# Decay exponents of a chunked scan: from TensorE matmuls to sums broadcast by DMA and clamped on GpSimd, with weight casts on ScalarE

## The reference

```python
proj = hidden_states @ in_proj_w.T
gate, xBC, dt = jnp.split(proj, [INTER, INTER + CONV_DIM], axis=-1)
xBC = silu(causal_conv_4_taps(xBC) + conv_b)
x, Bm, Cm = jnp.split(xBC, ...)
dt = jnp.clip(softplus(dt + dt_bias), DT_MIN, DT_MAX)
A = -jnp.arange(1, H + 1)
cs = jnp.cumsum(dt * A, axis=-1)              # within a chunk
Lmat = jnp.where(tri, jnp.exp(cs[l] - cs[s]), 0.0)
scores = (C[l] . B[s]) * Lmat
Ydiag = scores @ (x * dt)
# the second chunk also gets the first chunk's part, decayed by
# exp(cs_first[end] - cs_first[s]) * exp(cs_second[l])
Y = Ydiag + Yoff + x * D
yg = Y * silu(gate)
out = (yg / rms_per_group(yg)) * norm_w
return out @ out_proj_w.T
```

## Time and profile before

| What | Value |
| --- | --- |
| median of 3 runs | 2436.57 us (2436.28 to 2437.01) |
| time of the profiled execution | 2438.06 us |
| span of the profiled execution | 2436.3 us |
| TensorE busy | 2246.3 us, 92% |
| VectorE busy | 1789.6 us, 73% |
| ScalarE busy | 983.2 us, 40% |
| GpSimd busy | 842.5 us, 35% |
| the 64 units of stage C | about 695 to 2173 us of the span |

### The profile page before, as it was taken

How to read it: one execution, slowest core, us unless ns; L and a number is a source line. 1 busy time by engine, 2 the same in 40 slices (tenths; PEclk the granted TensorE clock), 3 DMA queues, 4 the chain that set the end, 5 groups by cost and what they waited for, 6 DMA issues and landing times. The chain is left out here.

```text
span 2436.3 us, 35643 instructions
## 1 busy us (share of the span) xinstructions
PE 2246.3 (92%) x11269; PEld 1731.1 (71%) x11333; DVE 1789.6 (73%) x2628; ACT 983.2 (40%) x1535; POOL 842.5 (35%) x481
## 2 busy tenths in 40 slices
PE   7888689979999999999999999999999999985987
PEld 5776568767867777776777777777777777764865
DVE  5433354448878887888888888888888888877887
ACT  2322111114344454554554455454455555431222
POOL 5424034321133443444335335334434435330000
PEclk9999889989999999999999999999999999996999
DMA  5413230012221111010111111111010110102433
GB/s 191 169 47 134 62 117 0 0 40 83 100 76 41 43 38 41 27 53 27 41 49 31 41 40 41 39 41 41 27 53 28 39 53 27 41 5 91 142 112 108
DMA packets 61935, 145.13 MB, mean 60 GB/s; under 512 B 15726, under 2 KB 18944, under 8 KB 61312
## 3 DMA queue, kind: packets, MB, share of 16 engines
q1 hardware_dynamic: 61888, 144.53, 18.0%
HBM read 133.74 MB, written 10.75 MB: 59 GB/s over the span
## 5 line engine op out<-in xcount | busy, mean ns | idle before, releaser
L70 PE MATMUL bank<-xT_hi,C_w_hi 128*128 128x512 f32 x1160 | 480.0, 414 | 13.4 <-POOL C_w_lo L1390 6.7
L71 PE MATMUL bank<-xT_lo,C_w_hi 128*128 128x512 f32 x1160 | 460.5, 397 | 0.0
L72 PE MATMUL bank<-xT_hi,C_w_lo 128*128 128x512 f32 x1160 | 459.9, 396 | 0.0
L1355 POOL TENSOR_TENSOR C_w_lo<-C_raw,C_w_hi 128x512 fp32r<-128x512 f32 x130 | 172.2, 1325 | 580.5 <-DVE C_w_hi L1182 530.1
L1109 DVE SCALAR_TENSOR_TENSOR C_acc<-bank,C_par,C_acc 128x510 f32<-128x510 f32 (+2 forms) x384 | 285.6, 747 | 68.9 <-ACT C_acc L1423 43.5
L1509 ACT ACTIVATE C_decay<-bank 128x512 f32<-128x512 f32 x384 | 215.8, 597 | 262.8 <-PE bank L1656 132.1
L1222 DVE TENSOR_TENSOR C_group_out<-bank,C_group_out 128x512 f32<-128x512 f32 x256 | 175.0, 684 | 176.6 <-PE bank L72 176.0
L1231 DVE TENSOR_TENSOR C_decay<-C_decay,C_cb 128x512 f32<-128x512 f32 x384 | 291.9, 789 | 4.2 <-DMA C_cb<-cb_rows 2.5
L70 PEld LDWEIGHTS bank<-xT_hi,C_w_hi 128*128 128x128 f32 x1160 | 219.3, 189 | 79.2 <-issue 10.8
L72 PEld LDWEIGHTS bank<-xT_hi,C_w_lo 128*128 128x128 f32 x1160 | 219.2, 189 | 53.2
L71 PEld LDWEIGHTS bank<-xT_lo,C_w_hi 128*128 128x128 f32 x1160 | 219.5, 189 | 48.1
(11 more groups left out here) (236 smaller groups left out, 4437.5 us busy)
## 6 DMA issues: line engine op xcount, KB each, us to landing
C_raw<-in_Cxg SPq DMA_DIRECT2D x65, 512.0 KB, 3.5
C_raw_out<-in_Cout SPq DMA_DIRECT2D x64, 256.0 KB, 3.4
D_raw<-in_D SPq DMA_DIRECT2D x32, 512.0 KB, 3.8
A_raw<-in_A SPq DMA_DIRECT2D x20, 512.0 KB, 5.9
A_stat_raw<-in_D SPq DMA_DIRECT2D x16, 512.0 KB, 3.5
D_raw<-in_D SPq DMA_DIRECT2D x32, 256.0 KB, 2.6
cb_rows<-C_decay SPq DMA_DIRECT2D x8, 768.0 KB, 3.3
C_cb<-cb_rows SPq DMA_DIRECT2D x8, 768.0 KB, 4.4
```

What stands on the lines that cost most here:

```text
L70: pe.matmul(out, lh, rh, start=start, stop=False)
L71: pe.matmul(out, lh, rl, start=False, stop=False)
L72: return pe.matmul(out, ll, rh, start=False, stop=stop)
L1355: e.tensor_tensor(w_lo[:, slot, :], raw_at, f32(w_hi[:, slot, :]), ALU.subtract).then_inc(lo_done, 1)
```

## The change

- The running sums cs (float32, 128 heads by 1024 tokens) are stored once in DRAM. For each unit one DMA (`load_cs`) reads the two heads' rows and writes them to all 128 partitions, 1 MB, into one of two buffers `cs_all`. The three small loads are gone.
- TensorE's exponent rounds, the mask matmuls and the bf16 parts are gone. GpSimd computes min(cs[l] - cs[s], 0) in 16 pieces of 128x128 per unit (`clamp`), straight into `decay`. For the first chunk against the second, ScalarE takes the broadcast sums with a bias per partition (8 Exp of 128x128); of the clamped pieces it makes 4 Exp of 128x512, in place. The mask is multiplied into the C.B blocks when they are made, once per group.
- GpSimd's low part of the x weights now stands inside `clamp`, after the wait for `inside` of the same unit.
- The three weight casts go from VectorE to ScalarE. ScalarE's exponentials stand ahead of the gate's Silu, and it copies the unit's own sums (`sums`).
- `turn` writes banks 6 and 7 and stands after the first output tile; `x_steps` stands after the first `out_add`. `in_g` waits for the gate's Silu of the unit before in place of `x_steps`.
- Before the units, three more transposes (of cs and of the sums to a chunk's end) and their copies, and five pieces in place of three in `move_cb`; the making of the bf16 parts is gone.

```diff
-        cs_rows = nc.dram_tensor("cs_rows", (P, 3, N), BF16, kind="Internal").ap()
-        cs_cols = nc.dram_tensor("cs_cols", (P, BATCH, 3, SEQ), BF16, kind="Internal").ap()
-        end_rows = nc.dram_tensor("end_rows", (P, 3, N), BF16, kind="Internal").ap()
+        cs_rows = nc.dram_tensor("cs_rows", (HEADS, N), F32, kind="Internal").ap()
...
-        left = sb("left", [P, 2, SEQ], BF16)
-        right = sb("right", [P, N], BF16)
-        fill = sb("fill", [P, 2 * SEQ], BF16)
+        cs_t = sb("cs_t", [P, CHUNKS, HEADS + 2])
+        cs_two = sb("cs_two", [P, 2, CHUNKS, 2])
+        end_t = sb("end_t", [P, BATCH, HEADS])
+        cs_all = sb("cs_all", [P, 2, 2 * N])
...
-            def load_rows(u):
-                heads = bass.ds(u.U * 2, 2)
-                wait(sp, S.seg_mm, u.U * ROUNDS)
+            def load_cs(u):
+
                 if u.first:
-                    sp.wait_ge(S.parts_out, 80)
-                    sp.wait_ge(S.fills_in, 128)
-                sp.dma_start(right[18:24, :], cs_rows[heads, :, :].rearrange("h a t -> (h a) t")).then_inc(S.rows_in, 16)
-                sp.dma_start(right[0:6, :], end_rows[heads, :, :].rearrange("h a t -> (h a) t")).then_inc(S.rows_in, 16)
-                sp.dma_start(left[6:18, :, :], cs_cols[heads, :, :, :].rearrange("h b a t -> (b a) h t"))\
-                  .then_inc(S.rows_in, 16)
+                    sp.wait_ge(S.cs_out, 16)
+                if not u.first_pair:
+                    sp.wait_ge(S.decays, (u.U - 1) * EXPS)
+                sp.dma_start(cs_all[:, u.j, :].rearrange("p (h t) -> p h t", h=2),
+                             cs_rows[bass.ds(u.U * 2, 2), :].unsqueeze(0).broadcast_to([P, 2, N])).then_inc(cs_in[u.j], 16)
...
-                for r in range(3):
-                    if r == 2:
-                        v.wait_ge(S.cb_mm, 2 * g + 2)
-                    v.tensor_copy(e[:, r, :], bank[4 + r][:, :]).then_inc(S.cb_moved, 1)
+                for bp in range(2):
+                    own = lambda t, c: t.rearrange("p (b c l) -> p b c l", b=2, c=2)[:, :, c, :]
+                    v.scalar_tensor_tensor(out=own(e[:, bp, :], 0), in0=mask[:, 0:2 * P].rearrange("p (b l) -> p b l", b=2),
+                                           scalar=0.0, in1=own(bank[4 + bp][:, :], 0), op0=ALU.is_ge, op1=ALU.mult)\
+                     .then_inc(S.cb_moved, 1)
+                    v.tensor_copy(own(e[:, bp, :], 1), own(bank[4 + bp][:, :], 1)).then_inc(S.cb_moved, 1)
+                v.wait_ge(S.cb_mm, 2 * g + 2)
+                v.scalar_tensor_tensor(out=e[:, 2, :], in0=mask[:, :], scalar=0.0, in1=bank[6][:, :],
+                                       op0=ALU.is_ge, op1=ALU.mult).then_inc(S.cb_moved, 1)
...
-                                bank[2 + h][:, :].rearrange("p (c h q) -> p c h q", c=4, h=2),
+                                bank[6 + h][:, :].rearrange("p (c h q) -> p c h q", c=4, h=2),
...
-                x_weights(U + 1, 1 - s)
-                if u.j == 0 and not u.first:
-                    out_weights(u)
...
-                gate_weights(U + 1, 1 - s)
+                x_steps(u, 0)
+                x_steps(u, 1)
                 if out:
                     out_add(u, 1)
                 decay_round(u, 0)
                 if out:
                     out_add(u, 2)
                 decay_round(u, 1)
+                decay_round(u, 4)
                 if out:
                     out_add(u, 3)
                 decay_round(u, 2)
-                x_steps(u, 0)
-                x_steps(u, 1)
                 decay_round(u, 3)
-                decay_round(u, 4)
                 decay_round(u, 5)
                 if u.group_ends:
                     mean_square(u, g)
-                if u.j == 1:
-                    out_weights(u)
             for_units(v, body)
-            out_weights(last)
             y_low(last.V - 1, 0, 1)
             for h in range(2):
...
+            def clamp(u):
+                wait(e, S.y_mm, u.U * 2)
+                if u.first:
+                    e.wait_ge(S.cb_stored0, 8 * GROUPS)
+                    e.wait_ge(S.cb_stored1, 8 * GROUPS)
+                e.wait_ge(S.sums_copied, u.U + 1)
+                e.wait_ge(cs_in[u.j], (u.U - u.j) * 8 + 16)
+                low(S.x_w_hi, 0, raw[:, 1 - u.j, 0:D], S.x_w_lo, u.U + 2)
+                for h in range(2):
+                    for c in range(2):
+                        for b in range(BATCH):
+                            at = N * h + SEQ * b + CHUNK * c
+                            to = decay[:, 4 + h, P * b:P * (b + 1)] if c else \
+                                decay[:, 2 * h + b // 2, SEQ * (b % 2):SEQ * (b % 2) + CHUNK]
+                            e.tensor_scalar(to, cs_all[:, u.j, at:at + CHUNK], cs_two[:, u.j, 2 * b + c, h:h + 1],
+                                            0.0, ALU.subtract, ALU.min).then_inc(S.clamped, 1)
             def body(u):
                 U, s = u.U, u.j
-                low(S.x_w_hi, 0, raw[:, 1 - s, 0:D], S.x_w_lo, U + 2)
                 if u.j == 0 and not u.first:
                     out_low(u)
+                clamp(u)
...
+            def chunk_ends():
+                a.wait_ge(S.dt_chain_v, DT_V)
+                for b in range(BATCH):
+                    t = SEQ * b
+                    a.activation(ends[:, CHUNK * b:CHUNK * (b + 1)], cs[:, t:t + CHUNK], ACT.Identity, scale=-1.0,
+                                 bias=cs[:, t + CHUNK - 1:t + CHUNK]).then_inc(S.dt_chain_a, 1)
+            def x_weights(U, slot):
+                a.wait_ge(raw_in[slot], (U - slot) * 8 + 16)
+                wait(a, S.in_x, U * 2)
+                a.activation(w_hi[:, 0, :], raw[:, slot, 0:D], ACT.Copy).then_inc(S.x_w_hi, 1)
+            def gate_weights(U, slot):
+                wait(a, S.in_g, U * 2)
+                a.activation(w_hi[:, 1, :], raw[:, slot, D:2 * D], ACT.Copy).then_inc(S.g_w_hi, 1)
+            def out_weights(u):
+                a.wait_ge(raw_out_in[1 - u.j], (u.V - (1 - u.j)) * 8 + 16)
+                if not u.first_pair:
+                    a.wait_ge(S.out_added, (u.U - 2 + u.j) * 4 + OUT0)
+                a.activation(out_hi[:, 1 - u.j, :], raw_out[:, 1 - u.j, :], ACT.Copy).then_inc(S.out_w_hi, 1)
...
+            def sums(U, slot):
+                wait(a, S.clamped, (U - 1) * 16)
+                a.activation(cs_two[:, slot, :, :], cs_t[:, :, bass.ds(U * 2, 2)], ACT.Copy).then_inc(S.sums_copied, 1)
...
-            def decay_exp(u, r):
-                a.wait_ge(S.seg_mm, u.U * ROUNDS + (r + 1))
-                if r == 0:
-                    wait(a, S.y_mm, u.U * 2)
-                    if u.first:
-                        a.wait_ge(S.cb_stored0, 8 * GROUPS)
-                        a.wait_ge(S.cb_stored1, 8 * GROUPS)
-                a.activation(decay[:, r, :], bank[6 + r % 2][:, :], ACT.Exp).then_inc(S.decays, 1)
+            def decay_exp(u):
+                for h in range(2):
+                    for b in range(BATCH):
+                        if h == b == 0:
+                            wait(a, S.y_mm, u.U * 2)
+                            if u.first:
+                                a.wait_ge(S.cb_stored0, 8 * GROUPS)
+                                a.wait_ge(S.cb_stored1, 8 * GROUPS)
+                            a.wait_ge(cs_in[u.j], (u.U - u.j) * 8 + 16)
+                        at = N * h + SEQ * b + CHUNK
+                        a.activation(decay[:, 2 * h + b // 2, SEQ * (b % 2) + CHUNK:SEQ * (b % 2 + 1)],
+                                     cs_all[:, u.j, at:at + CHUNK], ACT.Exp,
+                                     bias=end_t[:, b, bass.ds(u.U * 2 + h, 1)]).then_inc(S.decays, 1)
+                    first = decay[:, 2 * h:2 * h + 2, :].rearrange("p r (b c l) -> p (r b) c l", b=2, c=2)[:, :, 0, :]
+                    a.wait_ge(S.clamped, u.U * 16 + (8 * h + 4))
+                    a.activation(first, first, ACT.Exp).then_inc(S.decays, 1)
+                    a.wait_ge(S.clamped, u.U * 16 + (8 * h + 8))
+                    a.activation(decay[:, 4 + h, :], decay[:, 4 + h, :], ACT.Exp).then_inc(S.decays, 1)
...
                 if u.group_ended:
                     root(u.g)
+                if u.j == 0 and not u.first:
+                    out_weights(u)
                 x_tap(u, 0)
                 x_tap(u, 1)
+                x_weights(u.U + 1, 1 - u.j)
                 x_silu(u, 0)
                 x_silu(u, 1)
                 if not u.first:
                     y_high(u, 0)
+                decay_exp(u)
                 gate_silu(u, 0)
                 gate_silu(u, 1)
-                for r in range(ROUNDS):
-                    decay_exp(u, r)
+                gate_weights(u.U + 1, 1 - u.j)
                 if not u.first:
                     y_high(u, 1)
+                if u.j == 1:
+                    out_weights(u)
                 if u.group_ended:
...
-                    pe.wait_ge(S.xd_done, u.V * 2 + (h + 1))
+                    pe.wait_ge(S.g_silu, u.V * 2 + (h + 1))
```

(42 more changed lines are left out.)

131 lines of the change are left out of this document (48 added, 83 removed).

## The result

The changed kernel takes 2560.61 us (2558.15 to 2565.14), the kernel before 2436.79 in runs beside it; the ratio is 1.0508, 95% interval 1.049 to 1.0526. The forecast was 2410, the range ended at 2500. The profiled execution has a span of 2557.2 us.

What follows compares the result with a forecast made beforehand. TensorE was taken to bound the units, and after the change the SBUF access that GpSimd and VectorE share. From 2438 us, less 49 in the units, plus 21 at groups' ends, it forecast 2410, range 2310 to 2500.

Steps and rivals of the forecast that it cites:

- What it removes: On TensorE, the exponent matmuls go: 2.2 us per unit, 142 us in all, leaving a floor of about 20.6 us.
- the rival in which TensorE stays the bound: A clamp costs 0.29 us, so SBUF access by GpSimd and VectorE stays under TensorE's floor: 2319 us; chance 0.22.
- The broadcast and ScalarE's load: The 1 MB DMA per unit costs nothing; ScalarE gains 3.8 us per unit, to 15.7 of 22, not the bound.
- The clamp's price: On GpSimd, one clamp of 128 columns takes 0.40 us, between 0.29 and 0.54; 6.4 us per unit.
- The shared way: GpSimd and VectorE operations wait for each other at SBUF, so their work adds up: 22.0 us per unit, 49 us gained.
- the sum of 20.8 us: Per unit, GpSimd's and VectorE's contending SBUF work, clamps included; with 1.3 us unused it gives 22.1 us.
- slower by the clamps: Rival: a GpSimd clamp costs over 0.44 us; 2487 us at 0.50, some 2515 at 0.54; chance 0.32.
- Where TensorE idles: TensorE idles before `inside`, ended by a decay round, 1.4 us per unit.
- At a group's end: Late `squares_sum`, ScalarE's scalings and GpSimd's sums and memset cost 3 us more than the old 5.5, seven times: 21 us.
- units of 20.9 and 22.6 us: Limits of a unit's period in the forecast case, given as 2345 to 2432 us in total; chance 0.38.
- sixteen clamps of 0.50 us: On GpSimd, at this dearer price the layout ends at 23.2 us per unit, 2487 us in total.

Runs made afterwards that it cites:

- The wide subtraction of two tensors: Changed kernel with GpSimd's sixteen clamps made four two-input subtractions of 512 columns, ScalarE clamping by Relu before Exp of the negative: 2388.53 us, ratio 0.9796.
- the rounds off the shared way: Changed kernel with the six decay rounds of a unit reading a PSUM bank in place of the SBUF array of products: 2462.99 us, ratio 1.0105.
- the wide clamps: Changed kernel with the 16 clamps of 128 columns per unit made 4 of 512 on the same elements: 2436.05 us, ratio 1.0003.
- half on each of two engines: Changed kernel with the second head's eight clamps done on ScalarE as Relus, the first head's eight kept on GpSimd: 2378.83 us, ratio 0.9756.
- the ends rearranged: Half-and-half clamp version without the group output's memset, four tiles' scaling and adding one unit later, output-weight cast behind the first taps: 2352.65 us, ratio 0.966.

## Why the prediction was wrong, by its own steps

- **What it removes: right.** The floor was given as 20.6 us per unit; without the clamps the units take 20.5 and 20.72, and the time of 2321.54 is 2 us from the 2319 of the rival in which TensorE stays the bound, with 2 us more at a group's end as that rival had it (13 over seven).
- **The broadcast and ScalarE's load: right.** 6.8 us to landing, never waited for within the units. ScalarE has 121.67 us in a group, 15.2 per unit with the groups' scalings in it, against 15.7.
- **The clamp's price: the step that failed.** I took 0.40 us between 0.29 and 0.54; it is 0.71, and 0.77 from start to start on the mean. Both ends came from GpSimd operations of another kind: a memset (0.93 ns a column) and a two-tensor one (2.19). I took the two-tensor slope, with 0.09 us for the operand, as the high end, because a clamp "reads one stream". The measured slope is 3.34. The wide subtraction of two tensors shows it from the other side, 1.05 us at 512 columns where nothing holds it, against 1.99 for the clamp. The Trainium skill (GPSIMD Engine Reference, on engine selection) calls one-input work roughly line-rate; the trace does not agree for this one: VectorE does it in 278 ns.
- **The shared way: half right.** Rounds beside squares were forecast at 1.3 us or more and took 1.76, their mean rose as said, and taking them off that way gave back 98 us. But the sum of 20.8 us counted the clamps in it, and rounds beside clamps take 0.72. With the right price this sum would have been 20.8 + 16 x (0.77 - 0.40) + 1.3 = 28.0 us per unit; 23.7 were measured, so the clamps overlap with VectorE's work where I had added the two up. The Trainium skill (SBUF — State Buffer, Who interferes with whom) says that a VectorE instruction with two SBUF inputs contends with a GpSimd instruction that reads SBUF, which a clamp does. The trace agrees on one side only: the clamps wait for the rounds (0.99 against 0.71 us), the rounds hardly for the clamps (0.72 against 0.68). The two errors have opposite signs and hid each other in part; that the result lies only 60 us above the range is luck of that kind.
- **What bounds instead.** GpSimd's own queue with its wait for `inside`: per unit (179.45 - 8.6 of a group's end) / 8 = 21.4 us of work, and it may not begin the clamps until `inside` is through, which costs 5.0 us in the pair shown above (171.6 us in 25 waits in all). It was not among the rivals as such; the rival "slower by the clamps" had the right sign and cause, 0.32, but its dearest clamp was 0.54, so that the range ended under the result.
- **Where TensorE idles: wrong place.** I said 1.4 us per unit before `inside`; there it is 44.2 us in all, 0.7 per unit. The larger wait is one step on, at the output tile, behind `y_low`, 113.7 us. A late round also makes `y_high` and `y_low` late.
- **At a group's end: mis-sized.** 3 us more than before, against 8.3 (7.1 on the mean of the seven). Two of the mechanisms named were the ones in the timeline (scalings ahead of the tap, sums and memset ahead of the clamps), but they were taken at less than half their price; GpSimd was thought to have 6 us free in each unit. The third was not: `squares_sum` waits for GpSimd's sum of the squares (30.0 us in seven waits) and not for the third `out_add`.
- **The clock: left out.** The sum has no term for a lower clock. Against the run without clamps the same matmuls took 63 us longer, and the lower clock stands behind waits of ordinary units as well as of groups' ends.
- **Two small sums.** By the prediction's own terms units of 20.9 and 22.6 us give 2339 and 2448 us, not 2345 and 2432, and sixteen clamps of 0.50 us add 1.6 us to the unit of 22.0, not 1.2. Neither changes what was forecast.
- **Still open.** The 141 us that remain with the rounds off the shared way show as TensorE's waits behind `y_low` and the sum of the squares and the slower matmuls after them, but were not split further between GpSimd's load and the low parts, squares and gatings that meet on the same way; and the wide clamps (8.4 us in place of 12.4 per unit) came out at the old time, which is fitted by load and by position alike. A decision between them would need the order on GpSimd changed with the same load, which was not tried.

## What to carry to other kernels

Bound an unseen operation by rows of its own kind on its own engine; if there is none, let the range go far beyond the nearest other kind, because "fewer inputs" was no upper bound here. When work moves to an engine that shares a way with another, sort the operations by what the rows show each to hold and to be held by before adding them up, and ask where each will land beside which: shortening the harmless ones can push the harmful ones onto the critical ones. Give a wait of the matmul engine its price with the lower clock behind it. And put a piece of work where the engines' orders have a hole, in parts if need be: half on each of two engines gave 2.4%, and 3.4% with the ends rearranged; all on one engine gave nothing or a loss.
